# A four-layer decoder on one core: turned scores, chains per unit ordered by tables, and constant products placed by a table

## The reference, cut to what matters

```
x = x + L0_attn(ln(x));  x = x + L0_xattn(ln(x), ctx);  x = x + L0_ffn(ln(x))
x = x + L1_attn(ln(x));  x = x + L1_xattn(ln(x), ctx);  x = x + L1_ffn(ln(x))      # L1_ffn rounds by the maximum over the whole tensor
x = x + L2_attn(ln(x));  x = x + L2_xattn(ctx, ln(x));  x = x + L2_ffn(ln(x))
x = x + L3_attn(ln(x));  x = x + L3_xattn(ln(x), ctx);  x = x + L3_ffn(ln(x))

# L0_xattn, L1_attn, L3_xattn (16 heads of 8; L3_xattn with rotary angles), per sequence and head
attn = softmax(q @ k.T / sqrt(8));  out = (attn @ v) @ Wo + bo
# L1_xattn: the same, with the scores of the 16 heads mixed by a 16x16 matrix before the softmax
# L2_xattn: 16 heads of 64, queries from x, keys and values from the context and x together
# L3_attn: delta rule in chunks of 32 (an inverse of I - A per chunk), three causal filters of 3, 15 and 64 taps
#          on v, statistics of five paths -> gelu gate -> softmax over the paths -> mix -> rms norm
# L3_ffn: 8 experts, the two best by router, and a shared expert
```

## Time and profile before

| | |
|---|---|
| Runs | 1775.65, 1787.13, 1798.22 us; median 1787.13 |
| Profiled execution | 1792.9 us from its first instruction to its last |
| Prologue, part A, part B, part C | 28, 480, 111, 1174 us |
| TensorE, its weight loads, VectorE, ScalarE, GpSimd busy | 1530.7, 1300.6, 1100.9, 670.3, 127.9 us |
| Granted clock of TensorE, mean | 0.87 |
| Instructions | 40153 |

### The profile page before, as it was taken

One profiled execution on the slowest core, in us unless ns is written; L12 is line 12 of the kernel. 1 busy time (PEld: TensorE's weight loads), 2 busy tenths in 40 slices (PEclk: granted clock), 3 DMA queues, 4 the chain that ended last, 5 costly groups with the idle time before them and its releaser, 6 DMA issues. The chain is left out here.

```text
span 1792.9 us, 40153 instructions
## 1 busy us (share of the span) xinstructions
PE 1530.7 (85%) x17496; PEld 1300.6 (73%) x17496; DVE 1100.9 (61%) x2843; ACT 670.3 (37%) x1323; POOL 127.9 (7%) x265
## 2 busy tenths in 40 slices
PE   5888887898886899898879999779989977989986
PEld 3666676776654589797769788668879766978865
DVE  5668678577768566355658445567644565753565
ACT  4343463453547535222315323323422231532331
POOL 2010111111110000100000100000000000010000
PEclk8699998898997889898779988789988777998878
DMA  6000000000000100000000000000000000000000
GB/s 245 1 2 1 1 2 1 1 2 1 2 30 30 61 1 1 1 4 1 1 1 1 1 3 2 1 1 2 1 2 3 1 1 1 1 1 2 3 1 24
DMA packets 6510, 19.87 MB, mean 11 GB/s; under 512 B 2240, under 2 KB 4288, under 8 KB 5824
## 3 DMA queue, kind: packets, MB, share of 16 engines
q1 hardware_dynamic: 6336, 17.32, 2.7%
HBM read 16.27 MB, written 1.05 MB: 10 GB/s over the span
## 5 line engine op out<-in xcount | busy, mean ns | idle before, releaser
L480 PE MATMUL PS<-CC 128*128 128x256 f32 x656 | 197.1, 449 | 20.4 <-DVE mv L457 16.9
L480 PEld LDWEIGHTS PS<-CC 128*128 128x128 f32 x656 | 142.3, 229 | 45.7 <-DVE mv L457 17.7
L1839 PE MATMUL PS<-AR 64*64 64x32 f32 (+1 forms) x3072 | 124.3, 237 | 16.4 <-DVE AR L2112 8.5
L1839 PEld LDWEIGHTS PS<-AR 64*64 64x64 f32 x3072 | 121.5, 156 | 18.1 <-DVE AR L2112 9.0
L469 POOL TENSOR_SCALAR SC<-mv 128x2 f32<-128x2 f32 x96 | 18.6, 194 | 1568.9 <-DVE mv L457 1567.0
L587 PEld LDWEIGHTS PS<-vo,AR 128*64 128x64 f32 x2560 | 111.8, 178 | 25.1 <-issue 15.9
L587 PE MATMUL PS<-vo,AR 128*64 128x18 f32 x2560 | 121.4, 241 | 5.7 <-DVE AR L1493 3.9
L1855 PE MATMUL PS<-AR,PA 64*64 64x204 f32 (+39 forms) x2624 | 123.3, 323 | 2.8 <-issue 2.1
L567 PE MATMUL PS<-CC,AR 128*128 128x128 f32 x512 | 100.7, 343 | 19.9 <-ACT AR L551 19.9
L1855 PEld LDWEIGHTS PS<-AR,PA 64*64 64x64 f32 x2624 | 104.1, 144 | 10.7 <-issue 4.8
L531 DVE TENSOR_REDUCE SC<-PS 128x8 f32<-128x512 f32 x128 | 86.5, 684 | 21.8 <-PE PS L691 21.1
(11 more groups left out here) (405 smaller groups left out, 3114.3 us busy)
## 6 DMA issues: line engine op xcount, KB each, us to landing
WC<-in_cw SPq DMA_DIRECT2D x1, 5438.5 KB, 19.3
PA<-in_fd SPq DMA_DIRECT2D x1, 2624.0 KB, 9.9
PA<-in_stat SPq DMA_DIRECT2D x2, 1280.0 KB, 5.7
out<-X SPq DMA_DIRECT2D x1, 1024.0 KB, 5.1
PA<-in_aw SPq DMA_DIRECT2D x1, 975.0 KB, 10.8
AR<-in_raw SPq DMA_DIRECT2D x1, 832.0 KB, 7.5
CC<-in_const SPq DMA_DIRECT2D x1, 809.0 KB, 7.6
AR<-in_intw SPq DMA_DIRECT2D x1, 576.0 KB, 8.5
```

Of the source, the lines that this page charges most:

```text
L480: T.matmul(st.ps[:, bank, 0:ST], lhsT=ident, rhs=CC[:, 0:ST], start=True, stop=True)
L1839: m = T.matmul(ps[rows, bank, n * width:(n + 1) * width], lhsT=lhs[rows, n, :], rhs=rhs(rows, n), start=True, stop=True)
```

## The change

*Turned scores.* In L0x, L1a and L3x the scores are computed once as before, for their row maxima only. VectorE writes the maxima of all heads into a 128x128 tile (`vector_maxima`), TensorE transposes it, ScalarE copies it (`mt`). Then TensorE computes the scores again with queries and keys exchanged, so that the keys lie on the output's rows, and adds the negative maxima by a second product with a constant of -1 and 0 (`less`). ScalarE's exponential reads PSUM and writes the weights for `tensor_weigh` as they are needed.

```diff
+        def scalar_turned(st, k, scale):
+            yield
+            A.wait_ge(*st.pe.at(f"{k}.most"))
+            A.copy(st.mt[:, :], st.ps[:, 0, 0:P]).then_inc(*st.act.up(f"{k}.most"))
+            yield
+            AT = attention_parts(st)[1]
+            for r in range(GR):
+                A.wait_ge(*st.pe.at(f"{k}.below{r}"))
+                A.activation(AT[:, 512 * r:512 * r + 512], st.ps[:, r, :], ACT.Exp, scale=scale).then_inc(
+                    *st.act.up(f"{k}.exps{r}"))
+                yield
+
+        def tensor_turned(st, k, qm, km):
+            yield
+            T.wait_ge(*st.dve.at(f"{k}.most"))
+            T.transpose(st.ps[:, 0, 0:P], st.mx[:, :], ident).then_inc(*st.pe.up(f"{k}.most"))
+            yield
+            T.wait_ge(*st.act.at(f"{k}.most"))
+            strips = [(r, slice(32 * r, 32 * r + 32)) for r in range(GR)]
+            for q in range(SQ):
+                for r, rows in strips:
+                    T.matmul(st.ps[:, r, q * P:(q + 1) * P], lhsT=km[rows, q, :, :], rhs=qm[rows, q, :, :],
+                             start=True, stop=False)
+                for r, rows in strips:
+                    m = T.matmul(st.ps[:, r, q * P:(q + 1) * P], lhsT=cc("less")[rows, q * P:(q + 1) * P],
+                                 rhs=st.mt[rows, :], start=False, stop=True)
...
+            for r in range(GR):
+                if r == 0:
+                    T.wait_ge(*st.act.at(f"{k}.values1"))
+                T.wait_ge(*st.act.at(f"{k}.exps{r}"))
+                tensor_weigh(st, k, attention_parts(st)[1], r)
+                yield
```

```diff
-def take_turns(first, second, ahead, rounds):
...
+def take_turns(chains, turns):
+    for turn in turns:
+        steps, chain = divmod(turn, 10)
+        for _ in range(steps):
+            next(chains[chain])
...
+            for n, pair in enumerate(taps):
+                if n == 0:
+                    T.wait_ge(*a.at(f"{k}.v"))
+                    T.wait_ge(*a.at(f"{k}.local"))
+                    T.wait_ge(fd_there, 16)
...
+                if n % 3 == 2 and n < len(taps) - 2:
+                    yield
```

```diff
-        def keep_clock(st, bank, first, second):
-
-            for _ in range(second if st.s else first):
-                T.matmul(st.ps[:, bank, 0:ST], lhsT=ident, rhs=CC[:, 0:ST], start=True, stop=True)
+        def tensor_fill(banks):
+
+            for b in banks:
+                T.matmul(bank[int(b)][:, 0:P], lhsT=ident, rhs=CC[:, 0:P], start=True, stop=True)
+                yield
...
+        TURNS_C = {
+            "tensor": (21, 14, 20, 21, 20, 54, 11, 24, 10, 51, 50, 21, 24, 21, 20, 24, 20, 74, 31, 24, 21, 30, 11, 10,
...
+        for engine, part, aside in (("tensor", tensor_part_c, tensor_aside_c), ("scalar", scalar_part_c, scalar_aside_c),
+                                    ("vector", vector_part_c, vector_aside_c), ("pool", pool_part_c, None)):
+            fill = [tensor_fill(FILL_C)] if engine == "tensor" else []
+            chains = [part(st) for st in streams] + [aside(sd) for sd in asides if aside] + fill
+            take_turns(chains, TURNS_C[engine])
```

```diff
-            def both_norms():
-                for u in streams:
-                    V.wait_ge(*u.dve.at(f"{k}.norms"))
-                for _ in vector_rsqrt(b, SC[:, :, 32:48], SC[:, :, 16:32], SC[:, :, 256:272]):
-                    pass
...
+            yield from vector_rsqrt(v, sc[:, 32:48], sc[:, 16:32], sc[:, 256:272])
...
-            if st.s:
-                table_for(ACT.Gelu)
```

More of the change, by code:

```diff
@@ L152, in bc @@
     return u.to_broadcast(shape)
-def take_turns(first, second, ahead, rounds):
[L158 to L166, removed]
+def take_turns(chains, turns):
[3 more added lines that the diff above has]
+            next(chains[chain])
+    for chain in chains:
+        for _ in chain:
+            pass
 def decoder(nc, x, ctx_in, coords, const_d, aw_d, raw_d, intw_d, cw_d, stat_d, fd_d, out, known):
@@ L293, in all_done @@
                 for line in st.lines:
-                    line.n = 0
+                    line.count[0] = line.last = 0
         def vector_prologue():
@@ L1067, in decoder @@
                              ("pool", pool_part_a)):
-            take_turns(part(streams[0]), part(streams[1]), AHEAD_A[engine], NITER)
+            fill = [tensor_fill(FILL_A)] if engine == "tensor" else []
+            take_turns([part(st) for st in streams] + fill, TURNS_A[engine])
         all_done()
@@ L1079, in decoder @@
         XY = mybir.AxisListType.XY
-        bank = [PS[n // 4][:, n % 4, :] for n in range(8)]
         def chunk(t, c):
@@ L1504, in pool_l2_attention @@
             yield from pool_norm(st, "L2a")
-            for _ in range(5):
-                yield
-        LAG = {"scores": 1, "turn": 4, "weigh": 5, "out": 6}
-        JOBS = [(st, j) for j in range(TS * GR) for st in streams]
+            yield
+        NJOB = TS * GR
         class Cross:
@@ L1773, in pool_l2_ffn @@
                 *st.pool.up(f"{k}.xb"))
-            for _ in range(3):
-                yield
+            yield
         class Delta:
@@ L1955, in tensor_l3_attention @@
             yield
-            keep_clock(st, 0, 3, 0)
-            yield
-            T.wait_ge(*pair.dve.at(f"{k}.moments", st))
+            T.wait_ge(*v.at(f"{k}.all_moments"))
             for j in range(TS):
@@ L2487, in tensor_part_c, with scalar_aside_c @@
                 yield from tensor_l3_ffn(st)
+        def scalar_aside_c(sd):
+            for i in range(NITER):
+                begin(sd, "c", i)
+                yield from scalar_l2_cross_aside(sd)
+                yield from scalar_l3_attention_aside(sd)
         def scalar_part_c(st):
@@ L2498, in scalar_part_c, with vector_aside_c @@
                 yield from scalar_l3_ffn(st)
+        def vector_aside_c(sd):
+            for i in range(NITER):
+                begin(sd, "c", i)
+                yield from vector_l2_cross_aside(sd)
+                yield from vector_l3_attention_aside(sd)
         def vector_part_c(st):
```

661 lines of the change are left out of this document (318 added, 343 removed), and 131 rows, old and new, of tables (AHEAD_A, AHEAD_C, TURNS_A, TURNS_C).

## The result

The changed kernel takes 1536.23 us (median of 4 runs, 1531.35 to 1540.36), against 1783.64 us for the kernel before (median of 4, 1775.65 to 1798.22). The ratio is 0.8604, with a 95% interval of 0.856 to 0.8649. The forecast was 1636 us with a range of 1555 to 1740: the direction was right, and the gain was 247 us where I had 151.

The account below looks back on a forecast made before the run. The kernel was taken as bound by dependence chains with two dense stretches between them, not one engine. Terms -32 - 32 - 81 - 26 + 12 + 8 = -151 us on 1792.9 gave 1642, less 6: 1636 us, range 1555 to 1740.

Parts of the forecast that it names:

- Turned scores: Softmax attentions in A and C: shorter chain, 8 us per pair in C, half in A; -32 us each.
- Clock: TensorE's granted clock in A (0.90) and C (0.86): denser stages should raise it, wider products go; 0 taken.
- Own and side chains, order from tables: C: one unit's work hides the other's waits, -81 us; filter taps in the delta attention's tail, -26 us.
- my check: TensorE alone in C: about 1050 us, 867 of work and fill over clock 0.90, plus 87 of gaps.
- Split pairs: Small VectorE chains in C issued once per unit, 204 more instructions, 41 us less 22; hidden, 0 taken.
- Fill: A and C: 830 constant products, 207 us for the old 195, priced as if none lay in gaps; +12 us.
- Activation tables: ScalarE between the units' Gelu: 14 table switches for 8, six more at 1.28 us; +8 us at most.
- the good end: Best case for the clock: 0.95 in A and 0.90 in C, worth -58 us.
- Rival 4: The clock rises as well: -151 - 58, 1578 us; chance 0.08.
- Rivals 1 and 2: 1: only the head overlaps, 1726 us, chance 0.18. 2: the stagger gives nothing, 1807 us, chance 0.10.
- the head's 81: C: waits in the stages beside the cross attention, 20.2 us per iteration, hidden four times; -81 us.
- Rival 3: A and C: constant products stand before ready work, making the kernel slower, +75 + 8, 1870 us; chance 0.06.

Follow-up runs that it names:

- run 2: The kernel before without any of its constant products, order kept: 1871.14 us, ratio 1.0457.
- run 5: The changed kernel without constant products and with the old softmax in its three attentions, order kept but for three steps: 1741.49 us, ratio 0.9754.
- run 1: The changed kernel without its constant products, all other instructions and their order kept: 1621.84 us, ratio 0.9075.
- run 9: The changed kernel without constant products, the third part's filter products moved back to their places in the kernel before: 1713.77 us, ratio 0.9604.
- run 3: The kernel before with each constant product issued twice at the same places: 1853.88 us, ratio 1.0383.

## Why the forecast missed, step by step

**What the sum left out.** Of the 248 us that A and C lost by the table above, 129 are time in which TensorE did no work of use (idle time and products together, 415 to 286 us), where the sum had 151. Another 132 us are time that the lower clock had added, where the sum had 0, and the work takes 13 us more. So the waits were, if anything, priced too high, and the forecast missed by the step **Clock: 0 taken**.

**Turned scores (-64).** In the old order they earned nothing: +13 us in A, and in C no less idle time (158 us against 150). In the new order they are worth 92 us by the profiles, 69 of them in A, and 121 by the ratios. By the profiles' windows most of it is the clock (67 us, with 36 of idle time). The chain itself came out as worked out: no subtraction is left, and the forecast's prices give 11 us for a pair side by side and, an estimate, 8.6 for one unit alone (2.4 us for its four reductions instead of 4.8), where 8.2 and 12.5 were measured. (Unit 0's reductions have small steps of unit 1's feed-forward between them. And the 16 VectorE instructions in the earlier trace rows are 0.67 us apart, not the 0.60 that I used.) What failed is that I added its worth to that of the order: singly they give 0 us (with products) and 126 (without), together 247 (without).

**Own and side chains, order from tables (-81 and -26).** I counted the real-work-free time of two stages and half a tail; everything else was taken to stay. With the old softmax the order took 126 us off (run 2 to run 5), 92 of them idle time, so the sum of 107 was near. Whether for its own reasons isn't shown, and its split was off: the filters, which I had at -26, are worth 81 to 94 in this order. (The lead of unit 1, which I gave as up to 15 steps in C, goes up to 21 on TensorE by its table.) With the turned scores it took 247 us off where I had 171, and of that the lead and the places make nearly all: with the units in step my rule's tables come to 15 us. Idle time in C fell to 38 us, where my check asked for 87. The check was not consistent with the sum: it took 0.90 for the clock, while the sum took nothing from it. At 0.86 the same check asks for 1050 - 867 / 0.86 = 42 us of gaps. Split pairs: what they cost is in no run by itself; VectorE's busy time in C rose by 3 us though 22 us of subtractions went. By the code the units could not part without them, since each chain of the pair waits for both.

**Fill (+12).** 830 products as counted. They take 232 us, not 207, and cost nothing that shows: with half of them gone the kernel gains nothing. Each set in its own order, the new products earn 2 us more than the old ones, less than the runs can tell. So the +12 is not there, and most of the 232 us lie in time that would be idle: in A and C together TensorE's idle time is 234 us without them and 55 with them.

**Activation tables (+8).** 14 loads as counted (columns: busy us, mean ns, then idle time before):

```profile
L2162 ACT ACT_TABLE_LOAD x7 | 9.0, 1283 | 0.1
L2166 ACT ACT_TABLE_LOAD x7 | 9.0, 1283 | 0.1
```

They are 18 us of an engine that is busy for 41% of the span. The 1.28 us for one held; what they add to the kernel's time is in no run by itself. The Trainium skill (ScalarE: Activation LUTs, What ACT_TABLE_LOAD costs) gives 2.66 us for a switch, of which 1283 ns are the load and the rest a drain. This trace agrees on the load. It shows no drain: before the seven loads of a line ScalarE is idle for 0.1 us in all, and the activation starts 0.02 us behind the load (start, length):

```profile
733.00 1.28 ACT L2162 ACT_TABLE_LOAD   x1
734.30 0.84 ACT L2162 ACTIVATE AR<-PS,WC 128x256 f32<-128x256 f32 x2
```

**Clock (0).** This is the step that failed. The clock's share fell by 132 us, 103 of them in C, which is more than the 98 us between forecast and result. I had listed 0.95 and 0.90 as the good end; it is 0.99 and 0.97. I treated the clock as something that only the fill might change, and took the two to cancel. The runs show that it moved with the waits also where no product stands: from run 2 to run 1 idle time in C fell by 122 us and the clock's share by about 74 (0.18 x 966 against 0.11 x 905), and from run 1 to run 9 34 us more of idle time came with 42 us more from the clock. It is no fixed price: 71 us of idle time in C went with 0.97 in one run and 78.5 with 0.92 in another, and with products of 32 columns the idle time of A went (19 us) and the low clock stayed. What in a gap decides is open.

**Rivals.** Rival 4 had the right direction and less than half the size (58 us for 132). Rivals 1 and 2 did not come: A fell by 52 us, and C by more than twice the head's 81. Rival 3 did not come: with half of the fill left out the kernel is no faster. Something like it came in run 3, with the old products doubled, at +68 us. What the profile after was to show (C iterations of 255 to 270 us, clock under 0.92) was missed on the good side: the first three iterations take 234 to 242 us (TensorE's first instruction of L2a stands at 570.5, 804.3, 1040.3 and 1282.0).

**Open.** How much of the last 100 us in C, between my best table and the change's, is order within a unit and how much between units. What the turned scores are worth in an order made for the old softmax. And why nearly equal idle time went with different clocks.

## What to carry to other kernels

When dependence chains bound a kernel and TensorE's clock is below full, give the clock a term of its own in the sum: in the third part of this kernel, without products, each us of idle time that went or came moved 0.6 to 1.2 us of the clock's share with it, and the term that I left out is larger than my miss. Do not add the worth of a shorter chain to that of a new order: here they gave 0 and 126 us singly and 247 together, so ask of each step what will stand behind it. Try the partners apart, since in tables of one rule a small lead earned 73 us. Constant products were worth having where gaps remained (82 and 84 us in two kernels here). Half as many did nearly as well, they did not cover gaps that a changed order opened, and more of them at a few fixed places cost more than they gave.

## What the chip showed that I had not expected

Products of 32 columns did not hold the clock though TensorE was busy nearly all the time. A in the runs with 64 and with 32 columns, all other instructions the same:

```profile
33.30:468.90 435.60, 413.76 (x6338) 360.05 (x6337) 296.81 (x835) 179.62 (x392) 61.52 (x119) 0.99 0.02 5
```
```profile
33.40:530.20 496.80, 477.50 (x6337) 420.12 (x6337) 298.03 (x836) 179.68 (x392) 61.48 (x119) 0.84 0.02 4
```

Busy for 477.5 of 496.8 us, and the granted clock is 0.84, as with no products at all. (The profile models the ends of matrix products, so its busy time need not be time in which columns went through.) And a narrow product is hardly cheaper than a wide one (groups of the two runs, columns as above):

```profile
L493 PE MATMUL PS<-CC 128*128 128x64 f32 x1660 | 221.4, 277 | 0.0
```
```profile
L493 PE MATMUL PS<-CC 128*128 128x32 f32 x1660 | 251.5, 299 | 0.0
```

It is 232.1 us at 128 columns, 221.4 at 64, and 251.5 at 32 with the lower clock. Beside each product stands the load of its 128x128 weights. In the change these loads take nearly as long as the products:

```profile
L493 PE MATMUL PS<-CC 128*128 128x128 f32 x1660 | 232.1, 283 | 0.0
L493 PEld LDWEIGHTS PS<-CC 128*128 128x128 f32 x1660 | 211.0, 197 | 4.9 <-issue 0.3
```

That the loads set the pace is likely by these numbers, and no run separates it. So busy time as the page of the profile gives it did not tell whether the clock was held; the row with the granted clock did.
